# Layer-2 attention: context projections in the rounding stage, attention outputs scaled by VectorE from PSUM

## The reference

```
ln_out = _ln(hidden, ln_w, ln_b)
q  = _ln(fp8_linear(ln_out, wq,  q_in_scale))     # 16 heads of 128
k  = _ln(fp8_linear(ln_out, wk,  k_in_scale))     # 8 groups of 128
v  =     fp8_linear(ln_out, wv,  v_in_scale)
core = softmax(q k / sqrt(d)) v                   # self attention
qx = _ln(fp8_linear(ln_out, wqx, qx_in_scale))    # a second query, 16 heads
kx, vx = split(cond @ w_kv_x.T)                   # context: no fp8 rounding
kx = _ln(kx)
xout = softmax(qx kx / sqrt(d)) vx                # context attention
cat = clip(concat[core, xout] / proj_smooth, -448, 448), to bf16, to fp8
x = x + (cat @ wproj.T) * (proj_in_scale * proj_w_scale)
```

## Time and profile before

| | us |
|---|---|
| median of three runs | 1845.22 (1845.38, 1840.97, 1845.22) |
| profiled execution | 1841.28 |
| its span in the trace | 1839.5 |
| rounding stage | 871 to 905 |
| attention stage, to the last addition | 905.8 to 1313.3 |
| one batch in the steady part of it | 48.6 |

### The profile page before, as it was taken

One profiled execution on the slowest core, in us unless ns is written; L12 is line 12 of the kernel. 1 busy time (PEld: TensorE's weight loads), 2 busy tenths in 40 slices (PEclk: granted clock), 3 DMA queues, 4 the chain that ended last, 5 costly groups with the idle time before them and its releaser, 6 DMA issues. The chain is left out here.

```text
span 1839.5 us, 25081 instructions
## 1 busy us (share of the span) xinstructions
PE 1526.5 (83%) x8600; PEld 980.9 (53%) x8600; DVE 1081.8 (59%) x2306; ACT 806.6 (44%) x1881; POOL 785.3 (43%) x954
## 2 busy tenths in 40 slices
PE   6566659999797799998399999999699989836772
PEld 5322225566465356565167777777555565525662
DVE  5999972222674644354768888888722254562336
ACT  2898963111333211112588888888521111412221
POOL 1277741000200289792177777777310000027772
PEclk9666558999698899999599999999899988858886
DMA  2298861110503111310200000000111100056656
GB/s 78 60 183 178 179 146 61 41 35 26 183 2 129 53 58 60 121 55 23 80 2 1 1 1 1 1 1 2 44 30 43 35 25 1 33 205 233 230 171 238
DMA packets 174223, 140.12 MB, mean 76 GB/s; under 512 B 141793, under 2 KB 154721, under 8 KB 170386
## 3 DMA queue, kind: packets, MB, share of 16 engines
q1 hardware_dynamic: 165314, 114.89, 21.8%
q0 software_dynamic: 6416, 22.03, 3.5%
q10 hardware_dynamic: 2368, 1.61, 0.3%
HBM read 85.43 MB, written 19.50 MB: 57 GB/s over the span
## 5 line engine op out<-in xcount | busy, mean ns | idle before, releaser
L1848 POOL CAST l0m_pi<-l0m_pf 128x1024 bf16<-128x1024 int16 x128 | 133.2, 1040 | 107.5 <-ACT l0m_pf L1915 105.7
L389 PE MATMUL l1e_gu<-x_normT,l1e_w 128*128 128x512 f32 x384 | 171.6, 601 | 0.0
L1451 PE MATMUL l2x_pr<-l_w,l2x_xq 128*128 128x512 bf16 x576 | 141.8, 385 | 35.5 <-ACT credits L42 35.5
L1915 ACT ACTIVATE l0m_pf<-l0m_s,l0m_bias,l0x_sq 128x1024 int16<-128x1024 f32 x128 | 153.9, 1205 | 17.8 <-DVE l0m_bias L1946 11.3
L1942 DVE TENSOR_REDUCE l0m_mx<-l0m_s 128x1 f32<-128x1024 f32 x128 | 155.6, 1216 | 4.8 <-PE l0m_s L1857 4.4
L1857 PE MATMUL l0m_s<-l0x_kT,l0x_qT 64*128 64x512 bf16 x256 | 69.7, 561 | 68.4 <-ACT l0m_pf L1915 65.6
L389 PE MATMUL l0e_gu<-x_normT,l0e_w 128*128 128x512 f32 x272 | 121.3, 600 | 0.0
L1578 DVE BATCH_NORM_STATS2 l2x_bn<-l2x_raw 128x6 f32<-128x128 f32 x384 | 83.3, 279 | 64.3 <-ACT l2x_raw L1519 64.3
L389 PEld LDWEIGHTS l1e_gu<-x_normT,l1e_w 128*128 128x128 f32 x384 | 74.0, 194 | 84.3 <-issue 83.2
L389 PE MATMUL l2e_gu<-x_normT,l2e_w 128*128 128x512 f32 x256 | 114.3, 601 | 0.0
L441 ACT ACTIVATE l1e_sil<-l1e_gu 128x512 f32<-128x512 f32 x48 | 28.6, 596 | 178.6 <-PE l1e_gu L389 178.6
(11 more groups left out here) (508 smaller groups left out, 3602.0 us busy)
## 6 DMA issues: line engine op xcount, KB each, us to landing
l3m_w<-in_l_moe SPq DMA_DIRECT2D x16, 1280.0 KB, 6.8
l1e_w<-in_l_ffn SPq DMA_DIRECT2D x24, 384.0 KB, 3.1
l_rows<-zero_row SPq DMA_DIRECT2D x8, 1024.0 KB, 11.1
l_w<-l_rows SPq DMA_DIRECT2D x8, 1024.0 KB, 11.8
l0e_w<-in_l_ffn SPq DMA_DIRECT2D x17, 384.0 KB, 3.0
l2e_w<-in_l_ffn SPq DMA_DIRECT2D x16, 384.0 KB, 3.0
ctx_tok<-l_route SPq DMA_DIRECT2D x8, 512.0 KB
l2q_wps<-in_l_wp SPq DMA_DIRECT2D x16, 256.0 KB, 2.7
```

Of the source, the lines that this page charges most:

```text
L389: last = nc.tensor.matmul(gu[half][:, m, :], w[:, c % SW, (2 * k + m) * P:(2 * k + m + 1) * P], pg.xnT[:, k, cols(n)], start=(k == 0), sto ...
L1451: last = nc.tensor.matmul(flat(pr[t % 2][:]), src[:, k, tokens], pg.l2_w3[:, part, k, at:at + W], start=(k == 0 and part == 0), stop=(k == ...
L1848: nc.gpsimd.tensor_copy(pi[:, n % 8, :], pf[:, n % 4, :]).then_inc(s["rounded"], 1)
L1915: nc.scalar.activation(pf[:, n % 4, :], s_ps[n % 3][:], ACT.Exp, scale=sq[:, b, h:h + 1], bias=bias[:, n % 4:n % 4 + 1], accum_out=sm[:, b ...
```

## The change

**Context projections.** All 32 (8 batches by kx, kx, vx, vx) are computed in the rounding stage: TensorE runs them through eight PSUM buffers, ScalarE copies them out between its other copies (`keep_kv`), and GpSimd stores each to device memory (`l2_kv`) from a ring of four buffers. In the attention stage SP loads a batch's kx and vx back, into the memory of the context weight, which is spent by then, two batches deep. The context items lose slots 0, 1, 6 and 7 on TensorE and ScalarE; VectorE takes the statistics and the normalization of kx from the loaded tile.

**Attention outputs.** ScalarE's four reads go. VectorE multiplies the PSUM buffer of four heads by `rsmooth` in one `tensor_tensor` into the bf16 tile `z`, clamps `z` in place and rounds on. The buffer's release (`o_read`) is that product's.

```diff
+        KV_STEPS = 4 * B
+            kv = sb("kv", [P, 4, W])
+            kv_ps = [st.enter_context(nc.psum_tensor(f"l2q_kv_ps{i}", [P, W], F32)) for i in range(8)]
...
+            @block.tensor
+            def _(pe):
+                for i in range(KV_STEPS):
+                    b, u = divmod(i, 4)
+                    if i >= 8:
+                        pe.wait_ge(kv_kept, i - 7)
+                    for k in range(KD):
+                        last = nc.tensor.matmul(kv_ps[i % 8][:], pg.ctxT[:, k, b * P:(b + 1) * P], pg.l2_wx[:, k, u * W:(u + 1) * W],
+                                                start=(k == 0), stop=(k == KD - 1))
+                    last.then_inc(kv_done, 1)
+
+            @block.gpsimd
+            def _(pool):
+                for i in range(KV_STEPS):
+                    pool.wait_ge(kv_kept, i + 1)
+                    pool.dma_start(pg.l2_kv[i], kv[:, i % 4]).then_inc(kv_stored[i % 4], 16)
...
+                def keep_kv(i):
+                    act.wait_ge(kv_done, i + 1)
+                    if i >= 4:
+                        act.wait_ge(kv_stored[i % 4], 16 * (i // 4))
+                    nc.scalar.activation(kv[:, i % 4], kv_ps[i % 8][:], ACT.Copy).then_inc(kv_kept, 1)
...
                             keep(q)
+                            keep_kv(q)
                 keep(14)
                 keep(15)
+                for i in range(14, KV_STEPS):
+                    keep_kv(i)
...
-            v = pg.xnT
+            spent = pg.l2_wx[:].rearrange("p k n -> p (k n)")
+            kx = spent[:, 0:2048].rearrange("p (a u j d) -> p a u j d", a=2, u=2, j=U)
+            vx = spent[:, 2048:4096].rearrange("p (a n) -> p a n", a=2)
...
+            def projects(it, t):
+                return it is not None and (it[1] == 0 or 2 <= t < 6)
...
+            @block.sync
+            def _(sp):
+                for b in range(B):
+                    for i in range(4):
+                        sp.wait_ge(kv_stored[i], 16 * (b + 1))
+                    if b >= 2:
+                        sp.wait_ge(s["normed"], item((b - 2, 1)) * 6 + 2)
+                    for u in range(2):
+                        sp.dma_start(kx[:, b % 2, u], pg.l2_kv[4 * b + u].rearrange("p (j d) -> p j d", j=U)).then_inc(kx_in[b % 2], 16)
+                    if b >= 2:
+                        sp.wait_ge(s["valued"], item((b - 2, 1)) * 4 + 4)
+                    for u in range(2):
+                        sp.dma_start(vx[:, b % 2, u * W:(u + 1) * W], pg.l2_kv[4 * b + 2 + u]).then_inc(vx_in[b % 2], 16)
...
-                        if pi is not None and t < 8:
+                        if projects(pi, t):
...
-                                at = t * W if t < 2 else (t - 4) * W
-                                for k in range(KD):
-                                    last = nc.tensor.matmul(flat(pr[t % 2][:]), pg.ctxT[:, k, tokens], pg.l2_wx[:, k, at:at + W],
-                                                            start=(k == 0), stop=(k == KD - 1))
...
+                            if it[1]:
+                                pe.wait_ge(vx_in[it[0] % 2], 16 * 2 * (it[0] // 2 + 1))
...
-                        if job := due(t, 7, ai, zi, wi):
-                            it, a, m = job
-                            act.wait_ge(s["valued"], m + 1)
-                            act.wait_ge(s["widened"], m + 1)
-                            for j in range(U):
-                                h = it[1] * 16 + a * U + j
-                                last = nc.scalar.activation(of[:, a % 2, j, :], o_ps[:, j, :], ACT.Copy, scale=rsmooth[:, h:h + 1])
-                            last.then_inc(s["o_read"], 1)
...
+                            if projects(pi, t):
+                                dve.wait_ge(s["raw"], projected(pi, t) + 3)
+                                rows = raw[:, t]
+                            else:
+                                dve.wait_ge(kx_in[pi[0] % 2], 16 * 2 * (pi[0] // 2 + 1))
+                                rows = kx[:, pi[0] % 2, t]
...
-                            dve.wait_ge(s["o_read"], m + 2)
+                            dve.wait_ge(s["valued"], m + 1)
...
-                            ch.link(nc.vector.tensor_scalar(z[:], of[:, a % 2], 448.0, -448.0, ALU.min, ALU.max))
+                            h = it[1] * 16 + a * U
+                            nc.vector.tensor_tensor(z[:], o_ps[:], rsmooth[:, h:h + U].unsqueeze(2).to_broadcast([P, U, P]), ALU.mult)\
+                                .then_inc(s["o_read"], 1)
+                            dve.wait_ge(s["o_read"], m + 2)
+                            ch.link(nc.vector.tensor_scalar(z[:], z[:], 448.0, -448.0, ALU.min, ALU.max))
```

More of the change, by code:

```diff
@@ L1283, in attention_l2 @@
         wp_in = [pg.sem(f"l2q_wp_in{i}") for i in range(4)]
+        kv_done, kv_kept = pg.sem("l2q_kv_done"), pg.sem("l2q_kv_kept")
+        kv_stored = [pg.sem(f"l2q_kv_stored{i}") for i in range(4)]
+        KV_STEPS = 4 * B
         with ExitStack() as st:
@@ L1341, in attention_l2 @@
                  "recip", "p_normed", "p_turned", "p_kept", "valued", "o_read", "qsteps2", "widened", "quanted", "y_done", "y_added", "aff_in", "aggr", "y_scale", "smooth")
+        kx_in, vx_in = ([pg.sem(f"l2x_{m}_in{i}") for i in range(2)] for m in ("kx", "vx"))
         s = {m: pg.sem(f"l2x_{m}") for m in names}
@@ L1367, in attention_l2 @@
             wide = spare[:, 1024:2048].rearrange("p (a u n) -> p a u n", a=2, u=U)
-            of = spare[:, 0:1024].rearrange("p (a u n) -> p a u n", a=2, u=U)
             cq = sb("cq", [P, 4, U, P], BF16)
@@ L1441, in fn @@
                     for t in range(8):
-                        if pi is not None and t < 8:
+                        if projects(pi, t):
                             side = pi[1]
-                            pe.wait_ge(s["raw"], item(pi) * 8 + t + 1)
+                            pe.wait_ge(s["raw"], projected(pi, t) + 1)
                             tokens = slice(pi[0] * P, (pi[0] + 1) * P)
-                            if side == 0 or 2 <= t < 6:
-                                src = xq[:, (K_, K_, Q_, Q_, Q_, Q_, V_, V_)[t] if side == 0 else QX]
-                                at = t * W if side == 0 else 4096 + (t - 2) * W
-                                for k in range(KD):
-                                    for part in range(3):
-                                        last = nc.tensor.matmul(flat(pr[t % 2][:]), src[:, k, tokens], pg.l2_w3[:, part, k, at:at + W],
-                                                                start=(k == 0 and part == 0), stop=(k == KD - 1 and part == 2))
-                            else:
-                                at = t * W if t < 2 else (t - 4) * W
-                                for k in range(KD):
-                                    last = nc.tensor.matmul(flat(pr[t % 2][:]), pg.ctxT[:, k, tokens], pg.l2_wx[:, k, at:at + W],
-                                                            start=(k == 0), stop=(k == KD - 1))
+                            src = xq[:, (K_, K_, Q_, Q_, Q_, Q_, V_, V_)[t] if side == 0 else QX]
+                            at = t * W if side == 0 else 4096 + (t - 2) * W
+                            for k in range(KD):
+                                for part in range(3):
+                                    last = nc.tensor.matmul(flat(pr[t % 2][:]), src[:, k, tokens], pg.l2_w3[:, part, k, at:at + W],
+                                                            start=(k == 0 and part == 0), stop=(k == KD - 1 and part == 2))
                             last.then_inc(s["proj"], 1)
@@ L1506, in _ @@
                 pg.credit(nc.scalar, s["p_kept"], 1)
[L1507 removed]
                 act.wait_ge(s["aff_in"], 1)
[L1509 removed]
                 def fn(pi, ai, zi, wi):
                     for t in range(8):
[L1513 to L1519 removed]
+                        if projects(pi, t):
+                            act.wait_ge(s["proj"], projected(pi, t) + 1)
+                            which = (K_, K_, Q_, Q_, Q_, Q_, V_, V_)[t] if pi[1] == 0 else QX
+                            dst = flat(raw[:, t]) if t < 6 else pg.xnT[:, 0, (t - 6) * W:(t - 5) * W]
+                            nc.scalar.activation(dst, flat(pr[t % 2][:]), ACT.Copy, scale=scales[:, which:which + 1]).then_inc(s["raw"], 1)
                         if job := due(t, 3, ai, zi, wi):
@@ L1553, in _ @@
                 pg.credit(nc.vector, s["widened"], 2)
+                pg.credit(nc.vector, s["o_read"], 1)
                 for c in range(4):
```

31 lines of the change are left out of this document (15 added, 16 removed).

## The result

The changed kernel takes 1887.94 us (median of 4 runs, 1882.87 to 1888.14) against 1843.53 (4 runs): ratio 1.0227, 95% interval 1.0209 to 1.0246. It is slower, as forecast, by 44 us where 20 were forecast, and 6 us above the range.

The account below looks back on a forecast made before the run. TensorE was taken to bound the attention batch, 48.60 of 48.60 us busy. Terms 24.4 - 2.5 - 5 + 2.8 = +19.7 us on the mean 1843.2 gave 1863, range 1846 to 1882.

Parts of the forecast that it names:

- The rounding stage, +24.4 forecast: Rounding stage: 32 context projections outlast VectorE's rounding, so attention's first projection starts near 930.2 for 905.84; bounds +21.5 and +27.
- lose 2.5 us at a low clock: Start of the projections in the rounding stage: TensorE begins at a low clock, 2.5 us lost, 57.5 us in all.
- The stores were costed at nothing: Rounding stage: GpSimd's 32 stores cost nothing, since four buffers give 6.9 us a store where 256 KB loads take 2.7.
- It starts with TensorE just busy, so the 2.5 us go: Start of attention: TensorE comes straight from the projections, so the 2.5 us lost there at the low clock disappear, -2.5.
- The first context item, -5: First context item of attention: four projections removed, 6.9 us of TensorE, no wait added; -5, bounds 0 and -6.9.
- the ring: Steady batches: TensorE's next output waits for VectorE's product, which follows statistics of a projection behind the previous output; chance 0.63.
- The seven steady batches, +2.8: Attention's steady part: the added wait makes a batch 49.0 us for 48.6, 7 x 0.4; bounds -11.2 and +16.8.
- GpSimd in the ring: Rival for the steady batches: GpSimd's work delays VectorE's odd slots with a normalization, batch near 51, total 1879; chance 0.17.
- Late next is VectorE, which waits for projections that wait for VectorE: Steady batches: ScalarE's freed time buys nothing; VectorE is the next late engine, in a circular wait with TensorE's projections.
- the fast rival: Rival for the steady batches: no circular wait, VectorE's work alone bounds a batch, 45.5 or about 44, total 1828; chance 0.08.
- The product's price: VectorE's new product in attention: 0.689 us, from the experts' product of the same shape; bounds 0.60 and 0.82.
- the three signs of being wrong: Signs in the changed profile: a batch under 46 us, the rounding stage over 62, or the product over 0.9.

## Why the prediction was right and wrong

**The side and the mechanism were right.** The first edit lengthens the rounding stage beyond its cover, and the second closes a ring that takes the gain of the removed products: by the ratios, ScalarE's reading back gives 27 us, the product in front 36. Of the 21.9 us by which the span grew beyond the forecast, 13.9 arose in the batches, 5.1 between the first projection and the first addition, and 1.5 in the rounding stage.

**The rounding stage, +24.4 forecast, +25.9 measured: the sum within its bounds, two steps wrong in it, with opposite signs.** The projections were to lose 2.5 us at a low clock. They did not: TensorE had been idle for only 0.78 us before the first of them, and they take 55.17 us from there on, at clock 1.00. The stores were costed at nothing, with a cover that was argued for the copies into their buffers; that cover held, for TensorE never waits. What was overlooked is the exit of the stage behind them, which waits for GpSimd's queue: 3.35 us there. SyncE's stores take it away. That the sum came near is in part luck.

**"It starts with TensorE just busy, so the 2.5 us go": failed.** In the 5.5 us of the gap the clock falls, and attention starts low as before. The run with SyncE's stores starts high, as the step had it, but with 1.9 of its 3.8 us left at the first addition (3.5 at the eighth).

**The first context item, -5: about right.** The stretch to the first addition measured -2.4. With ScalarE reading, so that only the projections are gone, it is 87.4 us, 4.5 less than before. The product alone, in the kernel before, makes it 2.2 us longer (94.14 for 91.92). That the ring already works in the last part of this stretch was not in the sum.

**The seven steady batches, +2.8: the step that failed, +16.7 measured.** Five of the seven are steady and account for 13.5 of the 16.7. The eight steps of the ring, product start to product start, in the order of the forecast (self item into the slots 2, 4, 6, next 0; then the context item):

| | self 2 | 4 | 6 | next 0 | context 2 | 4 | 6 | next 0 | sum |
|---|---|---|---|---|---|---|---|---|---|
| forecast | 6.2 | 6.4 | 5.7 | 5.6 | 5.8 | 6.7 | 5.6 | 6.4 | 48.4 |
| after | 6.30 | 6.46 | 6.10 | 5.79 | 5.90 | 6.61 | 6.11 | 8.13 | 51.4 |
| slots filled | 6.28 | 6.48 | 6.10 | 5.79 | 5.88 | 6.63 | 6.09 | 6.46 | 49.7 |

Five steps are within 0.2 us, and a sixth with the slots filled. The miss of 2.4 us against the 49.0 taken is one large term and a small one. The large one is the step into the next slot 0: 8.13 us, and 6.46 with the idle slots filled. The sum priced every wait of TensorE at its length, and put at nothing what the waits can do to its clock, though it had the earlier trace rows with 0.55 in a stage where TensorE idles. The small one is the steps into the slots 6, 0.4 to 0.5 each: the normalization was put in at its free duration there and takes 1.08 us beside GpSimd's subtraction. The run with a quarter of the subtraction shows about half of this excess, 0.24 and 0.27 us, to be the subtraction's; the rest is open. It also took 0.4 off the step into slot 2 of the self item, whose forecast of 6.2 is therefore not shown to be right term by term. The rival "GpSimd in the ring" named this price for every odd slot with a normalization, and a batch of 51.0; that this comes near 51.4 is luck, since 1.7 us of it are the clock's.

**"Late next is VectorE, which waits for projections that wait for VectorE" held.** Of the waits in the four batches of the rows by line (total us, times, longest):
```profile
DVE l2x_bn L1624 <- ACT l2x_raw L1568: 13.7, 12, 2.3
PE l2x_o L1538 <- DVE l2x_z L1651: 9.3, 8, 1.3
```
VectorE's statistics wait for ScalarE's copy, TensorE's outputs for the product. And the fast rival, a batch bound by VectorE's work alone at 44 to 45.5 us, is the kernel with the product first: VectorE is busy 45.1 of 45.9 us.

**The product's price was right and its freedom is now shown.** 0.657 us on the mean, for 0.689 taken, and 0.68 beside GpSimd's subtraction for its whole length, where the normalization takes 1.09. The Trainium skill (GPSIMD Engine Reference, Specifications) has GpSimd contend with VectorE's instructions that have two SBUF inputs or are in a two-port mode; the runs agree, since the product (0.68 us) reads one operand from PSUM and the normalization (1.09) both from SBUF. The product also writes bf16 where the normalization writes 32-bit data, and no run separates the two. The Trainium skill (SBUF — State Buffer, SBUF: two separate sides) adds that whichever starts first holds the shared pair for its whole instruction; the trace agrees: GpSimd's subtraction ends at 1110.03, and the normalization that began at 1109.49 ends 0.55 us behind that, for the 0.69 us that it takes alone. The subtraction of 1.60 us that began behind a running normalization is the same the other way round.

Of the signs named, the first projection near 930 (932.0), the wait of TensorE's outputs for the product, and its price came. The clock was full at once where "after some 5 us" was named, the stage took 60.7 us for 58, TensorE was busy 45.2 of 51.4 us for 42 of 49, and the batch lay just above 47 to 51. None of the three signs of being wrong came.

## What to carry to other kernels

Before an instruction is moved from one engine to another, look at what stands ahead of it in the new engine's order, and put it in front if it frees a buffer: with the same work, its place was worth some 36 us here, and in the kernel before, at the front, the work itself cost nothing. Move into an idle stage only as much as the engine that sets that stage's end can hide (sixteen projections of 1.72 us behind 34 us of rounding cost nothing beside a run of the same chip without them, thirty-two cost 26, of which the exit behind GpSimd's stores is 3.8). And when an engine that was always busy gets gaps, price its clock too.

## What the runs showed of the hardware

- The exit of a stage whose GpSimd had issued stores came 4.2 us after ScalarE's last copy and 3.35 us after the last store was issued; with the same stores issued by SyncE all engines left 0.8 us after that copy.
- TensorE's clock fell to 1.2 GHz in each of five batches, in the middle of the stage; ahead of it stood two waits, of 0.87 and 1.31 us. One batch ahead of these, behind the same two waits, it stayed at 2.4 GHz. Products that nobody reads, 2.6 us of them in each batch, kept 2.4 GHz and made the batch 1.7 us shorter.
- One form of instruction on VectorE (two SBUF operands, 128x512) took 0.68, 1.08 or 1.53 us by what GpSimd was doing, while the product of the same shape, with one operand in PSUM and bf16 written, took 0.65 to 0.69 in every place.
